# Selective-scan blocks in another order: ScalarE's decay products first, one set of zero-weight products per place instead of two, and four more places

## What is computed

```python
def step(hst, ins):
    dt_t, B_t, C_t, x_t = ins
    dA = jnp.exp(dt_t[:, :, None] * A)
    hst = hst * dA + (dt_t * x_t)[:, :, None] * B_t[:, None, :]
    y_t = jnp.einsum('bds,bs->bd', hst, C_t)
    return (hst, y_t)
```

## Time and profile before

| | |
|---|---|
| median of 3 runs | 7117.57 us (7106.16 to 7133.88) |
| the profiled execution | 7129.15 us |
| its span | 7127.4 us |
| the scan stage in it, from 937 to 4763 us | 3826 us |
| mean granted clock of TensorE over the span | 0.893 |

### The profile page before, as it was taken

One profiled execution on the slowest core, in us unless ns is written; L12 is line 12 of the kernel. 1 busy time (PEld: TensorE's weight loads), 2 busy tenths in 40 slices (PEclk: granted clock), 3 DMA queues, 4 the chain that ended last, 5 costly groups with the idle time before them and its releaser, 6 DMA issues. The chain is left out here.

```text
span 7127.4 us, 201253 instructions
## 1 busy us (share of the span) xinstructions
PE 6456.8 (91%) x83760; PEld 3237.0 (45%) x83760; DVE 4213.0 (59%) x6974; ACT 4614.0 (65%) x9618; POOL 3332.5 (47%) x2816
## 2 busy tenths in 40 slices
PE   6888679999999999999999999979899999978988
PEld 3444434444444444444444444434345445444544
DVE  2555557676767666666666666655344445446554
ACT  3555478888888888888888888852144345345554
POOL 0011157666666666666666666650033223224432
PEclk8999878888888888888888888889999999989999
DMA  6555522222222222222222222235200000010000
GB/s 192 150 142 139 159 66 61 59 58 59 66 59 58 58 58 66 59 55 58 58 59 66 59 57 58 58 115 205 101 7 7 10 7 10 4 35 13 10 13 7
DMA packets 596348, 459.61 MB, mean 64 GB/s; under 512 B 449728, under 2 KB 504640, under 8 KB 577280
## 3 DMA queue, kind: packets, MB, share of 16 engines
q1 hardware_dynamic: 594624, 445.32, 21.6%
q10 hardware_dynamic: 832, 1.57, 0.1%
HBM read 301.29 MB, written 145.49 MB: 63 GB/s over the span
## 5 line engine op out<-in xcount | busy, mean ns | idle before, releaser
L1453 POOL TENSOR_TENSOR s_dec<-s_hs,s_dec 128x512 f32<-128x512 f32 x2040 | 2562.3, 1278 | 1219.4 <-DVE s_hs L1493 795.0
L1381 ACT ACTIVATE s_dec<-s_pa 128x512 f32<-128x512 f32 x4096 | 2267.5, 618 | 185.1 <-PE s_pa L1246 184.8
L1482 DVE TENSOR_TENSOR s_pA<-s_pA,s_dec 128x512 f32<-128x512 f32 x2040 | 1393.2, 695 | 792.5 <-ACT s_hs L1387 523.8
L1493 DVE TENSOR_TENSOR s_hs<-s_pB,s_dec 128x512 f32<-128x512 f32 x2040 | 1339.7, 685 | 333.2 <-PE s_py L1283 182.5
L1283 PE MATMUL s_py<-s_hs,s_cz 128*32 128x256 f32 x16384 | 1490.5, 443 | 0.0
L1387 ACT COPY s_hs<-s_pA 128x512 f32<-128x512 f32 x2048 | 1221.0, 597 | 375.1 <-PE s_pA L1256 373.4
L1292 PE MATMUL s_py<-s_still 128*32 128x512 bf16 x14840 | 1284.9, 422 | 0.0
L1246 PE MATMUL s_pa<-s_dl,s_al 18*128 18x64 bf16 x32768 | 1035.8, 198 | 77.1 <-DMA s_dl<-D 47.9
L1256 PE MATMUL s_pA<-az 18*128 18x256 bf16 x4096 | 814.2, 295 | 144.8 <-DVE s_pA L1482 128.6
L1256 PE MATMUL s_pB<-az 18*128 18x256 bf16 x4096 | 876.4, 296 | 35.7 <-DVE s_hs L1493 35.2
L1246 PEld LDWEIGHTS s_pa<-s_dl,s_al 18*128 18x128 bf16 x32768 | 770.8, 98 | 114.6 <-issue 51.0
(11 more groups left out here) (258 smaller groups left out, 6285.9 us busy)
## 6 DMA issues: line engine op xcount, KB each, us to landing
s_dl<-D SPq DMA_DIRECT2D x512, 144.0 KB
az<-U SPq DMA_DIRECT2D x1024, 72.0 KB
az<-B SPq DMA_DIRECT2D x1024, 36.0 KB
D<-p_dp SPq DMA_DIRECT2D x64, 384.0 KB, 5.8
U<-p_up SPq DMA_DIRECT2D x60, 384.0 KB, 6.3
B<-p_bz SPq DMA_DIRECT2D x144, 128.0 KB, 2.5
SZ<-p_sz SPq DMA_DIRECT2D x16, 1024.0 KB, 4.0
SK<-p_skip SPq DMA_DIRECT2D x16, 1024.0 KB, 5.8
```

The source lines that it names most:

```text
L1381: act.activation(dec[w][:].rearrange("p k i t d -> p (k i t) d")[:, :, DS * q + d:DS * q + d + 8], pa[:, bank, :].rearrange("p (d c) -> p ...
L1453: pool.tensor_tensor(m, two(hs[k][:, (x + 1) % 2, :]), m, ALU.mult).then_inc(m_done, 1)
L1482: dve.tensor_tensor(state, state, of_chunk(k, x), ALU.mult).then_inc(mul, 1)
L1493: dve.tensor_tensor(out, two(pB[:, k - 2, :]), of_chunk(k, x), ALU.add).then_inc(added, 1)
```

## The change

It has three parts, all in `body` of TensorE and ScalarE and in `keep_warm`.

1. `keep_warm` has one set of four products where it had two.
2. There are four more places in a body. At x = 0 and x = 8 one stands between pair 0 and the input products of part 0, which no longer are woven together. In round 1 two stand ahead of the input products for parts 2 and 3; they are added onto `pB`, behind the wait for the DVE addition that reads it, and the input product that follows overwrites `pB`. A body so has 33 x 4 = 132 zero-weight products where it had 29 x 8 = 232.
3. At x = 0 and x = 8 ACT makes pair 0 first, then copies part 0, makes pair 1, and copies part 1. The waits for DVE (`mul`, `added`) stand ahead of all of it.

```diff
-                def keep_warm():
+                def keep_warm(onto):
-                    for _ in range(2):
+                    for _ in range(1):
                         for k in range(CH):
-                            pe.matmul(py[QR * k:QR * (k + 1), :], still[:, W:W + QR], still[:, 0:W],
+                            pe.matmul(onto[QR * k:QR * (k + 1), :], still[:, W:W + QR], still[:, 0:W],
...
                         def to_b2(v):
+                            if late and v == 0:
+                                wait(pe, added, 2 * n + 1)
+                                keep_warm(pB[:, 0, :])
                             to_b(n + 1, (x + 1) % BODY, G + (x + 1) // BODY, 2, v)
-                        if more:
+                        if more and x % TB == 0:
+                            produce(G, x, 0, head, turn, None)
+                            if has:
+                                keep_warm(py)
+                            to_a0(0)
+                            to_a0(1)
+                        elif more:
                             produce(G, x, 0, head, turn, to_a0)
...
                         if ahead:
+                            if late:
+                                wait(pe, added, 2 * n + 2)
+                                keep_warm(pB[:, 1, :])
                             for v in range(2):
                                 to_b(n + 1, (x + 1) % BODY, G + (x + 1) // BODY, 3, v)
...
-                        copy_a(n, x, 0)
-                        if more:
-                            if x % TB == 0:
-                                wait(act, mul, 2 * n)
-                                wait(act, added, 2 * n)
+                        if more and x % TB == 0:
+                            wait(act, mul, 2 * n)
+                            wait(act, added, 2 * n)
                             take_pair(G, x, 0, head)
-                        copy_a(n, x, 1)
-                        if more:
+                            copy_a(n, x, 0)
                             take_pair(G, x, 1, head)
+                            copy_a(n, x, 1)
```

## The result

The changed kernel takes 7165.68 us (median of 12 runs, 7116.2 to 7280.86), the kernel before 7123.44 us beside it (12 runs, 7105.95 to 7149.3). The ratio is 1.0039, interval 1.0022 to 1.0057, and comes from ten of the 12 runs, since the two longest (7236.47 and 7280.86 us) count as slow ones: a little slower, where a little faster was forecast. That lies under the half per cent that the prediction called no change, but the interval lies wholly above one. The profiled execution took 7172.42 us, its span is 7170.7 us.

The account below looks back on a forecast made before the run. Bound: PE at the low clock, ACT's chain at full; the clock could move most. 53.4 + 0.7 + 0.1 + 0.64 - 0.46 - 0.14 = 54.2 us a body, plus 0.32 L (16), gave 59.3 us, 7085 us; range 6870 to 7350.

Parts of the forecast that it names:

- L: Low-clock time in a scan body, twice what the clock lacks: taken as 16 us after the change, against 18 before.
- The plain rounds: Scan rounds away from block starts: removing two sets saves nothing at full clock (3.02 us), 0.92 us at the low one.
- ACT's chain: Dependency chain through ACT in plain full-clock rounds: sets the 3.02 us; a round under 2.95 us would disprove it.
- The low round: Plain round at the low clock, bound by PE: 5.39 us falls to 4.47 us with two sets less.
- The block's first pair: ACT's pair 0 ahead of the copy at x = 0 and 8: free, saving 0.07 us each, 0.14 us a body.
- The late copy: Copy of part 1 behind pair 1 at block starts: costs 0.7 us in round 1, 0.1 us net at x = 9.
- The sum of 54.2 + 0.32 L: Whole scan body after the change: 54.2 us at full clock plus 0.32 us per low-level microsecond, 59.3 us.
- The two sets on `pB`: Added sets in round 1, hidden by nothing: 0.32 us each at full clock, 0.55 at low, 0.64 to 1.1 a body.
- case 12 to 20: Likeliest case, L between 12 and 20: 58.0 to 60.6 us a body, 7000 to 7170 us; chance 0.44.
- the upper bound: Upper side of L: thinner plain rounds and a fall at x = 8 lasting into the block's end, 20 to 34 us.
- rival 2: Single sets don't lift a fallen clock; plain rounds stay 4.47 us through a block, 7310 us (7170 to 7460); chance 0.28.
- The rule of the skill: Clock falls with PE idle gaps of some microseconds; if it held, the clock stays up throughout, 6760 us; chance 0.05.

Follow-up runs that it names:

- e13: The kernel before with no zero-weight products and the new order on PE and ACT at x = 0 and x = 8: 7476.32 us.
- e12: The kernel before with no zero-weight products at all, old order: 7358.28 us.
- e4: The changed kernel with both copies ahead of pair 1 on ACT at x = 0 and x = 8: 7218.56 us.
- e1: The kernel before with one set instead of two in its 29 places, nothing else: 6966.34 us.
- e5: The changed kernel without the two sets on `pB` in round 1: 7142.17 us.
- e8: e1 with three sets ahead of the input products of part 0 at x = 0 and x = 8: 6812.85 us.
- e9: e6 with three sets between pair 0 and the input products of part 0 at the block starts: 7386.45 us.
- e3: The changed kernel with the second set back in the 29 old places, one set in the four new ones: 7041.94 us.
- e11: e8 with three more sets on `py` in round 1: 6918.88 us.
- e14: e8 with a second set in rounds 2 and 3: 6964.92 us.
- e7: e1 with the two sets on `pB` in round 1: 7211.08 us.
- e6: The changed kernel with none of the four new places, so single sets and the new order: 7142.24 us.
- e2: The kernel before with the new order on PE and ACT at x = 0 and x = 8, two sets as before: 7212.46 us.

## Why the prediction failed

Its predicted time, 7085 us, was 81 us under the measured one. The stated range held the measured time, but the change went the other way: slower, where faster was forecast. The step that failed is L, the time at the low level: the second fall of the clock in a body was left out of it.

**The plain rounds: right.** At full clock ACT's chain was to hold, and it does: ACT is busy for 2.94 of 2.94 us. But the set did shorten it, by 0.08 us a round, and 2.94 us is a hair under the 2.95 us that I had named as proof against the chain. The rows say why it is not:

```profile
3174.66 1.13 ACT L1393 ACTIVATE s_dec<-s_pa 128x512 f32<-128x512 f32 x2
3175.69 0.58 ACT L1399 COPY s_hs<-s_pA 128x512 f32<-128x512 f32 x1
...
3175.35 0.11 PEld L1246 LDWEIGHTS s_pa<-s_dl,s_al 18*128 18x128 bf16 x4 [0.24 <-ACT s_dec L1393]
```

PE now waits 0.24 us for ACT, where before it had a set in hand. The copy stands 1.03 us behind the pair's start instead of 1.11: it had probably still waited a little for PE in what looked like a full ACT; no row shows that wait. My bound was too tight for that; "zero" should have been 0.08 us, some 0.8 us over ten or eleven rounds of a body. The low round was forecast at 4.47 us and is 4.59; the set is 0.40 us there instead of 0.46.

**The block's first pair: right.** Two exponentials fill ACT's wait, and the round ahead of the block start is 4.26 instead of 4.34 us, the 0.07 us forecast. That is so at full clock; at the low one it is longer by 0.34 us (e13 against e12).

**The late copy: the first term that was mis-sized.** I sized it at 0.7 us in round 1 and 0.1 us net in round 9. Round 9 takes 3.67 us against 3.26 before (below), so that the net is 0.41 us; against the old order with one set (2.94 us, e4) it is 0.73 us. I had let the set's saving cover nearly all of the delay, though PE then waits for DVE anyway.

```profile
3057.31:3060.57 3.26, 3.26 (x79) 1.68 (x74) 3.06 (x6) 3.05 (x7) 3.07 (x4) 1.00 0.21 84
```

At the low clock it is 1.18 and 0.91 us (e12, e13). The order with its gains is about 2 us a body there, where I had 0.66: some 90 us. It didn't show in full, because the single set gave more than I had counted. A line through the 63 bodies, length against L, is 51.1 us + 0.35 L for e1; my terms for the set alone give 53.4 - 0.46 = 52.9 us, 1.8 too much. After stands at 53.5 us + 0.33 L, so that order and places cost 2.4 us, where I had 1.3. The sum of 54.2 + 0.32 L came near by luck: two terms were wrong in opposite directions.

**The two sets on `pB`: right in size.** 0.64 to 1.1 us forecast, 1.03 us measured in round 1 at the low clock (after against e5).

**L: the step that failed.** I took 16 us, case 12 to 20, and measured 21.5. With that, 53.5 + 0.33 x 21.5 = 60.6 us a body, which is the mean measured; 0.7 us more than before, 64 times, is 45 us, and the profiled executions differ by 43. My own formula had named L above 18 as the point from which the change is a loss.

The 17 regular bodies have 2 x 0.12 x 58.08 = 13.9 us, well inside my case. For the body's first seven rounds the forecast holds, 15.4 us. What I left out of the 16 is the second fall, which brought 6.1 us in rounds 7 to 15. I had thought of one at the block start x = 8, but only for the upper bound, and had called round 9 nearly free. Both happen. In 13 bodies the clock falls behind the gap of 0.92 us in round 9, which the change itself makes; in 17 it falls in round 7 or 8, at the block start, which the change was to cover, against 10 before and 12 in e1.

Then rival 2's mechanism holds: plain rounds of 4.59 us, PE busy in all of them, for one or two rounds in most of these bodies, in a few to the end of the block. So rival 2 (chance 0.28) came true in part: in 31 of the 63 bodies L is above 20, and in ten of them it is 34 to 55 us, above my span of 20 to 34. The experiments show the parts of it: three sets in the block start take away the falls in rounds 7 and 8 (e8, e9), the early copy those in round 9 (e4), and e3, with two sets and the new places, has only one second fall in all, in round 8. Why one set at the block start, as in after and e5, doesn't suffice, and why some falls last a body long, stays open.

**The rule of the skill.** The Trainium skill, "TensorE: Matmul & The Clock Gate", section "Why this matters for your kernels", has the clock fall with idle gaps of some microseconds. Here it fell behind gaps of 0.92 us (round 9) and 0.40 us (x = 8), and no longer one lies between round 1 and these falls. So the traces don't agree with it. The part of it that says to keep the engine fed is borne out by e8, where 0.83 us of products in a gap of 1.27 us are worth 153 us against e1 (2.7% by the ratios, 190 us); e11 and e14 show its limit.

## What to carry to other kernels

Read the clock before the engines: where it is mixed, a change is worth what it does to the time at the low level first, and the mean clock of a stage hides a few bodies that carry the loss; look at their spread. When an instruction is moved ahead of another, cost the one left behind on every round where its reader has no slack, without setting against it a gain that can be had alone. And take such a change apart before keeping it: here one part alone was worth 2%, with one cheap filler in an existing gap 4.5%, and the three parts together were a loss.

## What the runs showed of the hardware

The clock's return is not in proportion to the work given. Two more sets in round 1 put it off to x = 5 in nearly all bodies (e7 against e1), three sets in the block starts of the new order raise L from 23 to 31 us (e9 against e6), and three more in round 1 of e8 give both bodies that are never low, 52.37 us, and some of 68.85 us. Nor does the length of a gap alone tell whether the clock falls: before, PE waits 1.04 us at a block start and the clock falls in round 8 in 10 bodies; in e2 it waits 0.71 us and the clock falls in 59. The bodies repeat to 0.02 us (61.80 us twelve times in e1, 58.08 us seventeen times in after), so I take it that the pattern follows from when in the stream of work a fall comes, and that small shifts of it change whole blocks; no run here shows that by itself. The spread of after's 12 runs is one of the clock too: the shortest, 7116.2 us, has a mean clock of 0.888, the longest, 7280.86 us, one of 0.855. By twice what the clock lacks that is about 520 us more at the low level for 165 us more time, 0.32 us for each, the slope of the bodies. With no zero-weight products at all most bodies are low from end to end, 64.06 us with PE busy for 62.43 us (e12). The products before, 232 a body, compute nothing and were worth 7358 - 7126 = 232 us of the whole.
